# A graph layer and a state space layer, stage one: one projection for B and C, all matmuls over 128 rows and outputs, halves added ahead of the layer norms' sums, one over the deviation in PSUM

## The reference

```python
# layer 0, graph part
msg = layernorm(x) @ W + B
sens = exp(-(1/adj - 1)**2 / (2 * 0.5**2)); weights = where(adj < 1.0, sens, 0.0)
x = x + weights @ msg
# layer 0, mamba2 block on layernorm(x)
z, xBC, dt = split(x @ W_in, [512, 1152])            # 512 + 640 + 8
xBC = silu(conv1d(xBC, 4 taps) + conv_b)
xh, B, C = split(xBC, [512, 576])                    # 512 + 64 + 64
dt = softplus(dt + dt_bias); A = -exp(A_log)
# in chunks: Y = (C B^T * decays) (xh * dt) + C h * decays + xh * D;  h = h * decay + B^T (xh * dt * decays)
Y = Y * silu(z); Y = Y * rsqrt(mean(Y*Y) + eps) * norm_w
x = x + (Y @ W_out) @ W_lin + b_lin
# layer 1: x + mamba1(layernorm(relu(adj @ layernorm(x) @ gcn_w + gcn_b))), then a top-2 mixture of experts
```

## Time and profile before

| | |
|---|---|
| median of 3 runs | 2886.9 us (2885.34 to 2891.23) |
| profiled execution, its own time | 2887.87 us |
| its span | 2885.8 us |
| mean granted TensorE clock | 0.937 |
| PE busy | 2505.6 us (87%) |
| DVE busy | 2119.0 us (73%) |
| ACT busy | 1348.4 us (47%) |
| POOL busy | 961.7 us (33%) |
| stage one, up to the last block's end | 1274 us |

### The profile page before, as it was taken

One profiled execution on the slowest core, in us unless ns is written; L12 is line 12 of the kernel. 1 busy time (PEld: TensorE's weight loads), 2 busy tenths in 40 slices (PEclk: granted clock), 3 DMA queues, 4 the chain that ended last, 5 costly groups with the idle time before them and its releaser, 6 DMA issues.

```text
span 2885.8 us, 24290 instructions
## 1 busy us (share of the span) xinstructions
PE 2505.6 (87%) x8262; PEld 1277.1 (44%) x8262; DVE 2119.0 (73%) x2426; ACT 1348.4 (47%) x1935; POOL 961.7 (33%) x723
## 2 busy tenths in 40 slices
...
DMA packets 68412, 221.03 MB, mean 77 GB/s; under 512 B 7570, under 2 KB 7826, under 8 KB 67906
## 3 DMA queue, kind: packets, MB, share of 16 engines
...
q10 hardware_dynamic: 544, 1.05, 0.1%
...
## 4 chain that ended last, share of the span: by engine, by line
PE 51%; DVE 27%; issue 14%; ACT 6%; POOL 1%; DMA 1%; DVEq 0%; SPq 0%; ACTq 0%; POOLq 0%
PE ps L535 13%; DVE h L1265 9%; DVE acc L1239 7%; PE ps L558 5%; ACT th L1432 2%; PE ps L807 2%; PE ps L654 2%; PE ps L686 2%; PE ps L585 2%; PE ps L587 1%; PE ps L621 1%; PE ps L638 1%; PE ps L643 1%; DVE u L1182 1%; DVE wgt L966 1%
## 5 line engine op out<-in xcount | busy, mean ns | idle before, releaser
L1935 POOL TENSOR_TENSOR dB<-du,bc 128x512 f32<-128x512 f32 x512 | 649.3, 1273 | 559.2 <-DVE h L1265 556.4
L1265 DVE TENSOR_TENSOR_SCAN h<-ps,hst,dB 128x512 f32<-128x512 f32 x512 | 649.3, 1273 | 13.7 <-POOL dB L1935 6.6
L1432 ACT ACTIVATE ps<-dt,cols 128x512 f32<-128x512 f32 x512 | 350.9, 688 | 442.5 <-DVE h L1265 438.3
L535 PE MATMUL ps<-wgt,msg 128*128 128x512 f32 x1024 | 530.7, 621 | 23.0 <-DVE wgt L971 22.6
L558 PE MATMUL ps<-raw,msg 128*128 128x512 f32 x1024 | 543.4, 623 | 3.0 <-DMA msg<-tmp_m 3.0
L807 PE MATMUL ps<-consts,h 128*128 128x128 f32 x2048 | 353.5, 302 | 211.2 <-DVE acc L1239 196.9
L807 PEld LDWEIGHTS ps<-consts,h 128*128 128x128 f32 x2048 | 263.2, 153 | 531.9 <-DVE acc L1239 368.1
L1239 DVE SCALAR_TENSOR_TENSOR acc<-ps,Ct,acc 128x512 f32<-128x512 f32 x450 | 326.7, 726 | 8.9 <-PE ps L807 8.9
L535 PEld LDWEIGHTS ps<-wgt,msg 128*128 128x128 f32 x1024 | 184.2, 194 | 254.8 <-issue 200.7
L1432 ACT ACTIVATE wgt<-wgt 128x1024 f32<-128x1024 f32 x256 | 258.1, 1047 | 38.2 <-DVE wgt L966 35.7
L558 PEld LDWEIGHTS ps<-raw,msg 128*128 128x128 f32 x1024 | 176.5, 199 | 127.8 <-issue 127.0
...
## 6 DMA issues: line engine op xcount, KB each, us to landing
raw<-in_adjT SPq DMA_DIRECT2D x256, 512.0 KB, 3.6
...
```

Of the source, the lines that this page charges most:

```text
L535: x = e.matmul(P[d][:, :], msg[:, j, d * 128:(d + 1) * 128], wgt[g % NW][:, l, :], start=j == 0, stop=j == NJ - 1)
L1265: e.tensor_tensor_scan(hr[n % 3][:, m, :], PS[4 + k % 2].t[:, :], dBr[k % 4][:, :], hst[:, n % 16, m:m + 1], ALU.mult, ALU.add).then_inc(S ...
L1432: return e.activation(out, in_, func, bias=bias, scale=scale)
L1935: e.tensor_tensor(dBr[k % 4][:, :], du[:, m, :], bcr[i % 3][:, n % 2, :], ALU.mult).then_inc(S("dB"), 1)
```

## The change

Four things, all in stage one.

1. B and C are projected together: m = 4 is one group of 128 outputs, B in partitions 0 to 63 and C in 64 to 127. One convolution and one tanh (128x512 in place of 64x1024) serve both; the silu is two operations of 64x512 that write B to `cc[0:64, 4]` and C to `cc[0:64, 5]`. The taps of C are copied once beside those of B.
2. All matmuls go over 128 rows and outputs: `cc[64:128, 5]` is zeroed once, the state `h0` has 128 rows, `bn` 128 columns, and the transposition of B, the product of C and B, C times the state and the new state use the full height. `NPA` goes from 60 to 55.
3. DVE adds the two halves of x, and of the squares, ahead of each layer norm's sums, and PE takes one matmul for each sum (`norm_a`).
4. ACT's Ln and Exp work in place in the PSUM bank of the variance (`norm_b`), and DVE's multiplication reads it there and frees it.

The norms of `messages` and of the later stages are as before.

```diff
...
-        xbc = sb(cA, "xbc", [128, 6, TB + 3])
+        xbc = sb(cA, "xbc", [128, 5, TB + 3])
...
-        bns = [sb(cA, f"bn{i}", [128, 64]) for i in range(2)]
+        bns = [sb(cA, f"bn{i}", [128, 128]) for i in range(2)]
...
-        h0 = sb(cA, "hs0", [64, 512])
+        h0 = sb(cA, "hs0", [128, 512])
...
-        NP, NPA, NSA, NPB, NPO = 64, 60, 62, 56, 18
+        NP, NPA, NSA, NPB, NPO = 64, 55, 62, 56, 18
...
+            def norm_a(x, sq_, m, v, summed, squared):
+                w.wait_ge(*summed)
+                w.wait_ge(m.evac, m.n - 1)
+                e.matmul(m.ps[:, :], avg, x, start=True, stop=True).then_inc(m.full, 1)
+                yield from [None] * 5
+                w.wait_ge(*squared)
+                w.wait_ge(v.evac, v.n - 1)
+                e.matmul(v.ps[:, :], avg, sq_, start=True, stop=True).then_inc(v.full, 1)
...
-                yield from norm(xbs[ib % 3], sq, pre_use(ib, 0), pre_use(ib, 1),
-                                [(prod[k].use(ib).evac, prod[k].use(ib).n) for k in range(2)], (S("sq"), ib + 1))
+                v = pre_use(ib, 1)
+                yield from norm_a(rr[:, :], sq[:, 0, :], pre_use(ib, 0), v, (S("xsum"), ib + 1), (S("sqsum"), ib + 1))
                 b = pre_use(ib, 2)
-                w.wait_ge(S("xn"), ib + 1)
+                w.wait_ge(v.evac, v.n)
...
-                for m in range(6):
-                    wd = 128 if m < 4 else 64
-                    c0 = 512 + 128 * m if m < 4 else 1024 + 64 * (m - 4)
+                for m in range(5):
+                    c0 = 512 + 128 * m
                     b = x_use(ib, m)
                     w.wait_ge(b.evac, b.n - 1)
-                    e.matmul(b.ps[0:wd, :], Win[:, 0, c0:c0 + wd], xc[:, 0, :], start=True, stop=False)
-                    yield
-                    e.matmul(b.ps[0:wd, :], Win[:, 1, c0:c0 + wd], xc[:, 1, :], start=False, stop=True).then_inc(b.full, 1)
+                    e.matmul(b.ps[:, :], Win[:, 0, c0:c0 + 128], xc[:, 0, :], start=True, stop=False)
+                    yield
+                    e.matmul(b.ps[:, :], Win[:, 1, c0:c0 + 128], xc[:, 1, :], start=False, stop=True).then_inc(b.full, 1)
...
-                    e.transpose(b.ps[:, 0:64], cc[0:64, 4, ts_], ident[0:64, 0:64])
-                    e.matmul(b.ps[:, 128:256], cc[0:64, 4, ts_], cc[0:64, 5, ts_], start=True, stop=True).then_inc(b.full, 1)
+                    e.transpose(b.ps[:, 0:128], cc[:, 4, ts_], ident)
+                    w.wait_ge(S("zero"), 3)
+                    e.matmul(b.ps[:, 128:256], cc[:, 4, ts_], cc[:, 5, ts_], start=True, stop=True).then_inc(b.full, 1)
...
-                    e.matmul(Yo.ps[:, :], cc[0:64, 5, ts_], h0[:, :], start=True, stop=True).then_inc(Yo.full, 1)
+                    e.matmul(Yo.ps[:, :], cc[:, 5, ts_], h0[:, :], start=True, stop=True).then_inc(Yo.full, 1)
...
-                    e.matmul(St.ps[0:64, :], bn[:, :], xdec[:, :], start=True, stop=True).then_inc(St.full, 1)
+                    e.matmul(St.ps[:, :], bn[:, :], xdec[:, :], start=True, stop=True).then_inc(St.full, 1)
...
-                x2 = ssd_use(ib, 34)
-                yield from norm(xbs[ib % 3], z[:, 2:4, :], ssd_use(ib, 35), ssd_use(ib, 36), [(x2.evac, x2.n)], (S("sq2"), ib + 1))
-                w.wait_ge(S("x2n"), ib + 1)
+                v = ssd_use(ib, 36)
+                yield from norm_a(tmp[:, :], z[:, 2, :], ssd_use(ib, 35), v, (S("xsum2"), ib + 1), (S("sqsum2"), ib + 1))
+                w.wait_ge(v.evac, v.n)
...
+                for k in range(2):
+                    w.wait_ge(prod[k].use(ib).evac, prod[k].use(ib).n)
+                e.tensor_tensor(rr[:, :], xbs[b][:, 0, :], xbs[b][:, 1, :], ALU.add).then_inc(S("xsum"), 1)
...
-                yield from (None, None, None, None, None)
-                w.wait_ge(S("rr"), ib + 1)
-                e.tensor_tensor(xc[:, :, :], xc[:, :, :], two(rr), ALU.mult).then_inc(S("xn"), 1)
+                yield from (None, None)
+                w.wait_ge(S("sq"), ib + 1)
+                e.tensor_tensor(sq[:, 0, :], sq[:, 0, :], sq[:, 1, :], ALU.add).then_inc(S("sqsum"), 1)
+                yield from (None, None, None)
+                v = pre_use(ib, 1)
+                w.wait_ge(S("rr"), 2 * ib + 2)
+                e.tensor_tensor(xc[:, :, :], xc[:, :, :], two(v.ps), ALU.mult).then_inc(v.evac, 1)
...
-                n_sil = 5 * ib
-                for m in range(6):
-                    wd = 128 if m < 4 else 64
-                    c, at = cc[0:wd, m, :], 24 * ib + 4 * m
+                for m in range(5):
+                    c, at = cc[:, m, :], 20 * ib + 4 * m
                     yield from (None, None, None)
                     b = x_use(ib, m)
                     w.wait_ge(b.evac, b.n)
-                    e.tensor_scalar(c, xbc[0:wd, m, 0:TB], col("cw0", 4 * m)[0:wd, :], col("cb0", m)[0:wd, :], ALU.mult,
-                                    ALU.add).then_inc(S("conv"), 1)
+                    w.wait_ge(S("taps"), 2)
+                    e.tensor_scalar(c, xbc[:, m, 0:TB], col("cw0", 4 * m), col("cb0", m), ALU.mult, ALU.add).then_inc(S("conv"), 1)
                     for k in range(1, 4):
                         w.wait_ge(S("conv"), at + k)
-                        e.scalar_tensor_tensor(c, xbc[0:wd, m, k:k + TB], col("cw0", 4 * m + k)[0:wd, :], c, ALU.mult,
...
+                w.wait_ge(S("tanh"), 5 * ib + 5)
+                for i in range(2):
+                    e.scalar_tensor_tensor(cc[0:64, 4 + i, :], th[64 * i:64 * i + 64, 0, :], 1.0, cc[64 * i:64 * i + 64, 4, :], ALU.add,
+                                           ALU.mult).then_inc(S("sil"), 1)
...
-                    e.tensor_copy(bn[:, :], b.ps[:, 0:64]).then_inc(S("bn"), 1)
+                    e.tensor_copy(bn[:, :], b.ps[:, 0:128]).then_inc(S("bn"), 1)
...
-                m = ssd_use(ib, 35)
+                m, v, x2 = ssd_use(ib, 35), ssd_use(ib, 36), ssd_use(ib, 34)
+                w.wait_ge(x2.evac, x2.n)
+                w.wait_ge(S("ms"), 4 * ib + 4)
+                e.tensor_tensor(tmp[:, :], xb[:, 0, :], xb[:, 1, :], ALU.add).then_inc(S("xsum2"), 1)
                 yield from (None, None)
                 w.wait_ge(m.full, m.n)
-                x2 = ssd_use(ib, 34)
-                w.wait_ge(x2.evac, x2.n)
                 e.tensor_tensor(z[:, 0:2, :], xb[:, :, :], two(m.ps), ALU.subtract).then_inc(m.evac, 1)
-                yield from (None, None, None, None, None)
-                w.wait_ge(S("rr2"), ib + 1)
-                e.tensor_tensor(z[:, 0:2, :], z[:, 0:2, :], two(tmp), ALU.mult).then_inc(S("x2n"), 1)
+                yield from (None, None)
+                w.wait_ge(S("sq2"), ib + 1)
+                e.tensor_tensor(z[:, 2, :], z[:, 2, :], z[:, 3, :], ALU.add).then_inc(S("sqsum2"), 1)
+                yield from (None, None, None)
+                w.wait_ge(S("rr2"), 2 * ib + 2)
+                e.tensor_tensor(z[:, 0:2, :], z[:, 0:2, :], two(v.ps), ALU.mult).then_inc(v.evac, 1)
...
+            def norm_b(xc_, sq_, m, v, squared, ln, n):
+                yield from (None, None, None)
+                w.wait_ge(m.evac, m.n)
+                act(sq_, xc_, ACT.Square).then_inc(squared, 1)
+                yield from (None, None, None)
+                w.wait_ge(v.full, v.n)
+                act(v.ps[:, :], v.ps[:, :], ACT.Ln, bias=EPS).then_inc(ln, 1)
+                w.wait_ge(ln, 2 * n - 1)
+                act(v.ps[:, :], v.ps[:, :], ACT.Exp, scale=-0.5).then_inc(ln, 1)
+                yield from (None, None)
...
+            w.wait_ge(S("zero"), 1)
+            e.memset(ccs[1][64:128, 5, :], 0.0).then_inc(S("zero"), 1)
...
-                w.wait_ge(S("conv"), 24 * ib + 24)
-                e.tensor_copy(xbc[:, 0:4, 0:3], xbc[:, 0:4, TB:TB + 3]).then_inc(S("halo"), 1)
-                e.tensor_copy(xbc[0:64, 4:6, 0:3], xbc[0:64, 4:6, TB:TB + 3]).then_inc(S("halo"), 1)
+                w.wait_ge(S("conv"), 20 * ib + 20)
+                w.wait_ge(S("zero"), 3)
+                e.tensor_copy(xbc[:, :, 0:3], xbc[:, :, TB:TB + 3]).then_inc(S("halo"), 1)
...
+            e.memset(ccs[0][64:128, 5, :], 0.0).then_inc(S("zero"), 1)
...
```

More of the change, by code:

```diff
@@ L596, in pre_a @@
                     yield
-                    if m % 2:
-                        yield from [None] * (4 if m < 4 else 2)
+                    yield from [None] * (4 if m % 2 else 2 if m == 4 else 0)
             def ssd(ib):
@@ L1043, in pre_a @@
                     if m % 2:
-                        for what in [cc[0:wd, m - 1:m + 1, :]] + ([z[:, m - 1:m + 1, :]] if m < 4 else []):
+                        for i, what in enumerate((cc[:, m - 1:m + 1, :], z[:, m - 1:m + 1, :])):
                             yield
-                            tz = (th, sq)[(n_sil - 5 * ib) % 2]
-                            n_sil += 1
-                            w.wait_ge(S("tanh"), n_sil)
-                            e.scalar_tensor_tensor(what, tz[0:wd, :, :], 1.0, what, ALU.add, ALU.mult).then_inc(S("sil"), 1)
```

(15 more changed lines are left out.)

44 lines of the change are left out of this document (27 added, 17 removed).

## The result

The changed kernel took 2826.7 us (median of 4 runs, 2823.8 to 2828.0) against 2889.0 for the kernel before (4 runs): the ratio is 0.978, 95% interval 0.977 to 0.980. That is 62 us less, where 44 were forecast; the time lies inside the stated range, and the gain at the very edge of what was counted as the forecast (25 to 62) and what as rival 1 (over 62). The span of the profiled execution is 2825.3 us, 60.5 less than before.

The account below looks back on a forecast made before the run. Stage one's blocks were taken as bound by TensorE, busy 799 of 823 us. Six steady blocks at 4.8 us (28.8), first phase 7.0, block 6 4.5 and block 7 3.5 give 43.8 off 2886.9: 2843.1 us, range 2812 to 2874.

Parts of the forecast that it names:

- rival 1: All PE work removed comes out as time, 2801 us; gains over 62 us belong here; chance 0.14.
- Work on PE: Matmul work removed: 4.7 us per pre and 6.0 per ssd, 10.8 a block, 86 us in all.
- (b): Full 128 rows and outputs in the ssd: 2.9 us from two matmuls and 1.4 from inner groups, per ssd.
- (a): B and C projected together: four narrow matmuls become two full ones, 3.0 us per pre, 8 times.
- Start of a block: Up to L638: 2.4 us of work removed comes back as waits, gain 0; bounds +2.4 and -1.3.
- Middle: Between start and tail of a block: narrow-matmul extras and a 1.4 us wait for weights go, gain 6.2 us.
- Tail: End of a block: 3.6 us of work removed, 4.0 of waits added, net -0.4, between +3.6 and -2.
- Clock: One more slow stretch in ten blocks and 0.65 us shifted, -1.0 us per block; bounds 0 and three more per block.
- First phase: One pre beside one product: 4.7 us of work and two table loads fewer, less 0.3 for adds, gain 7.0.
- Block 6: 10.8 us of work removed where 10.2 are idle already: gain 4.5 us, between 0 and 10.8.
- Block 7: No next pre, so only the full rows and outputs gain there: 3.5 us.
- Part (d): One over the deviation in PSUM: multiplication takes 1.22 us instead of 1.85; no change taken for Ln and Exp.

Follow-up runs that it names:

- the run on (b): Changed kernel with C times state and C times B over 64 rows, new state and B's transposition with 64 outputs again: 2857.6 us.
- (a) on PE: Changed kernel with B and C projected by four matmuls of 64 outputs, convolution, tanh and silu still joined: 2842.0 us.
- (c): Changed kernel with two matmuls for each mean and variance again and no adds of halves on DVE: 2831.6 us.
- (d): Changed kernel with Ln and Exp writing to SBUF again and the multiplications reading it there: 2859.2 us.

## Why the prediction was right, and where its size was off

The direction and the mechanism held; the sum was 18 us short. The blocks decide between the forecast and rival 1, which the total doesn't: blocks 1 to 5 took 130.2 to 132.2 us, where the forecast had 131.5 and rival 1 had 126.

*Work on PE.* 0.36 us for each narrow matmul: shown by the run on (b), to the hundredth. For (a), four narrow ones in pairs cost 13.5 us over six blocks, 2.3 a block, where 2.4 were expected of pairs; the 3.0 of the prediction, for four that stand alone, rests on the earlier trace rows and wasn't run. The sums' matmuls went as stated, 0.86 us each from start to start.

*Start of a block*, forecast 0: 1.5 us longer. The waits came as stated: 3.1 for the mean (forecast 3.2), 0.9 (0.95, though for POOL's rdA at L631 and not for the variance), 1.5 (1.8). What I missed is that the clock falls behind the 3.1 us wait (0.74 over 500 to 505 us). It is just past the stated bound of 1.3.

```profile
500.00:505.00 5.00, 5.00 (x16) 2.99 (x15) 2.25 (x4) 0.24 (x1) 1.04 (x1) 0.74 0.14 56
```

*Middle*, forecast 6.2: 7.3, of which about 1.3 is clock; so 6.0.

*Tail*, forecast -0.4: measured -0.4, with 1.7, 0.3 and 1.5 us of waits for 1.9, 0.7 and 1.4.

*Clock*, forecast -1.0 per block: this is the step that failed, in its sign. With every window of 5 us below 0.97 summed as (1 - clock) x 5, the six blocks lost 32 us before and 24 after: +1.4 per block. Per block 4.8 were forecast and 6.9 measured; without the clock 5.8 and 5.5. The waits and the work were thus sized well, and what lifted the gain over the forecast in the six blocks is clock that nobody had forecast: luck, as far as the prediction goes. I had taken, one stretch in one block, as the rule; blocks 1, 4 and 5 of the kernel before were 1.5 to 3.2 us longer than the one I read, because they had more of them; block 0 was 8 us longer, 5 of these in its first wait.

*First phase*, forecast 7.0: 12.9, of which 6.5 is the clock (0.94 over 107.8 us before, 1.00 after). 6.4 remain, near the 7.0; table loads went from eight to six.

*Block 6*, forecast 4.5: 2.6, with some 5 us more lost to the clock than before. *Block 7*, forecast 3.5: 3.3, with some 2 us more lost to it.

*Part (d)* was costed at the operand's 0.65 us. The runs show that its place among the others was worth 32 us, about half of them clock: it keeps DVE ahead of POOL's E once the starts are later. My sum was right here by luck: it left the two L985 at their old length without asking who would be issued first.

Undone one at a time, (a) on PE, (b), (c) and (d) cost 15, 31, 5 and 32 us, 83 in all, more than the 62 of the four together: they aren't additive. Some 40 of the 83 are clock in the profiled executions (21 for (b), 19 for (d)).

What stays open: why the clock falls behind one wait and not behind another like it. The traces show each fall, not a rule.
